# One-hot counts by groups of five destinations in a graph attention and expert kernel

## The reference

```
h = layernorm(x) @ W + b_w
e = leaky_relu(s_dst[dst] + s_src[src] + b_a);  w = exp(e)     # one score per edge
out[n] = sum of w * h[src] over the edges into n, divided by the sum of w
x = x + out
x = x + two of eight experts per node, weighted (hidden 256, gelu)
```

## Time and profile before

| | us |
|---|---|
| median of three runs | 764.05 |
| the profiled execution | 764.43 |
| its span, first to last instruction | 762.7 |
| PE busy | 676.3 |
| DVE busy | 549.9 |
| ACT busy | 461.4 |
| POOL busy | 284.8 |

### The profile page before, as it was taken

One profiled execution on the slowest core, in us unless ns is written; L12 is line 12 of the kernel. 1 busy time (PEld: TensorE's weight loads), 2 busy tenths in 40 slices (PEclk: granted clock), 3 DMA queues, 4 the chain that ended last, 5 costly groups with the idle time before them and its releaser, 6 DMA issues.

```text
span 762.7 us, 15157 instructions
## 1 busy us (share of the span) xinstructions
PE 676.3 (89%) x3518; PEld 527.3 (69%) x3519; DVE 549.9 (72%) x1510; ACT 461.4 (60%) x1227; POOL 284.8 (37%) x427
## 2 busy tenths in 40 slices
PE   3579964999999999999999999998789999999992
PEld 2457752777777777777777777776448788888881
DVE  4997778999998889989898989852694333333331
ACT  2245886788877888777777767720544455545551
POOL 2156720022222222222221212212233877777764
PEclk9798987999999999999999999999789999999997
DMA  8153000000010010101010101002912777777766
GB/s 321 48 181 126 1 1 1 16 29 29 29 57 29 25 33 28 56 28 55 29 55 29 55 29 55 29 29 98 390 50 57 139 130 133 132 127 130 138 121 81
DMA packets 29078, 59.72 MB, mean 78 GB/s; under 512 B 3792, under 2 KB 8272, under 8 KB 28752
## 3 DMA queue, kind: packets, MB, share of 16 engines
q0 software_dynamic: 10176, 24.12, 17.4%
q1 hardware_dynamic: 18400, 34.37, 12.6%
q10 hardware_dynamic: 432, 0.52, 0.2%
HBM read 35.93 MB, written 23.07 MB: 77 GB/s over the span
## 4 chain that ended last, share of the span: by engine, by line
PE 50%; DMA 10%; issue 6%; DVE 4%; POOL 2%; POOLq 2%; ACT 0%; DVEq 0%
PE ps L782 10%; PE ps L796 10%; PE ps L783 10%; DMA out_dram<-y,si 9%; PE ps L741 7%; PE ps L886 3%; PE ps L900 2%; PE ps L768 2%; PE ps L752 2%; PE ps L827 1%; PE ps L761 1%; PE ps L876 1%; DVE hot_r L1537 1%; POOLq L603 1%; POOL xg L623 1%
## 5 line engine op out<-in xcount | busy, mean ns | idle before, releaser
L1022 ACT ACTIVATE weight<-sdst_b,ss 128x125 f32 (+1 forms) x380 | 112.5, 388 | 84.1 <-DVE A_lo L1368 84.1
L782 PE MATMUL ps<-H_hi,A_hi 128*125 128x512 f32 x400 | 161.3, 403 | 0.9 <-DVE x_all L1382 0.9
L783 PE MATMUL ps<-H_lo,A_hi 128*125 128x512 f32 x400 | 157.9, 395 | 0.0
L1307 DVE TENSOR_SCALAR hot_k<-lane_k,key_t 128x250 bf16<-128x250 bf16 x600 | 121.0, 283 | 2.2 <-DVE weight_sum L1356 0.2
L532 POOL TENSOR_SCALAR seed<-seed 128x1 f32<-128x1 f32 x20 | 4.2, 212 | 308.7 <-DVE seed L1409 308.7
L1030 ACT ACTIVATE weight<-weight,ss 128x125 f32<-128x125 f32 x380 | 114.0, 388 | 0.0
L796 PE MATMUL ps<-H_hi,A_lo 128*125 128x512 f32 x400 | 105.0, 402 | 0.0
L782 PEld LDWEIGHTS ps<-H_hi,A_hi 128*125 128x125 f32 x400 | 74.2, 185 | 18.6 <-DVE x_all L1382 1.4
L783 PEld LDWEIGHTS ps<-H_lo,A_hi 128*125 128x125 f32 x400 | 74.3, 186 | 17.0
L886 PE MATMUL ps<-W_e,xgT 128*128 x352 | 83.4, 380 | 0.0
L796 PEld LDWEIGHTS ps<-H_hi,A_lo 128*125 128x125 f32 x400 | 71.5, 186 | 15.9
(11 more groups left out here) (238 smaller groups left out, 1186.6 us busy)
## 6 DMA issues: line engine op xcount, KB each, us to landing
W_e<-in_L_ffn_W_dram SPq DMA_DIRECT2D x16, 512.0 KB, 4.5
xf<-in_x_cols_dram SPq DMA_DIRECT2D x10, 512.0 KB, 3.8
x_all<-in_x_dram SPq DMA_DIRECT2D x20, 256.0 KB, 4.0
out_dram<-x_all SPq DMA_DIRECT2D x20, 256.0 KB, 2.0
xn_table<-xn SPq DMA_DIRECT2D x20, 256.0 KB, 2.3
b_b<-in_L_ffn_b_dram SPq DMA_DIRECT2D x1, 2048.0 KB, 8.9
Wf<-in_L_gnn_W_dram SPq DMA_DIRECT2D x1, 1024.0 KB, 6.1
b_b<-in_L_ffn_b_dram SPq DMA_DIRECT2D x1, 1024.0 KB, 13.8
```

The costliest lines, as they stand in the source:

```text
L782: pe.matmul(ps_agg[0:TN, :], A_hi[:, k, :], H_hi[:, k, :], start=(k == 0), stop=False)
L783: m = pe.matmul(ps_agg[0:TN, :], A_hi[:, k, :], H_lo[:, k, :], start=False, stop=False)
L1022: m = nc.scalar.activation(weight[s][:, k, :], dst_scores, ACT.Relu, bias=ss[:, 0, k:k + 1])
L1307: return nc.vector.tensor_scalar(into, lane_k[:, :], float(HW * h), key, ALU.add, ALU.is_equal)
```

## The change

Counts are made by groups ("windows") of five destinations, 25 to a tile and 500 in all. Each window has one slot of 128 edges, and one matmul of 100 columns (5 destinations by 20 source tiles) counts it. A tile with a window of more than 128 edges has its slots emptied and is counted chunk by chunk by the extra path. The slots are filled during the feature products: DVE searches each window's first chunk, POOL gathers that chunk for 500 windows (4 indirect loads of 125 rows of 128 edges), DVE finds the first edge in it, POOL gathers 128 edges from there (4 more), and DVE, PE (transposes) and ACT bring source lane and key of all slots into `lo2` and `key2`, lanes down, windows across. Per tile DVE then writes `hot_l` and `hot_k` with one comparison each. The additions over the source tiles go from DVE to POOL. PE counts 24 windows ahead of a tile's sums and the 25th, with the extra path's branch, after five pairs of them; the count of tile 1 moves behind the high part of tile 0, those of tiles 2 and 3 go into the high parts of tiles 1 and 2, and tile 1's sum goes to another PSUM bank. ACT makes its score copies between the high weights of tile 0. The loads of the edges move behind ACT's first feature copy.

```diff
+    WN = 5
+    WIN = TN // WN
+    WC = WN * NT
...
+            def window_rows(k):
+                pool.wait_ge(idx_ok, k + 1)
+                for g in range(WG):
+                    nc.gpsimd.indirect_dma_start(
+                        out=rows_w[0:WP, g, :, :].rearrange("p e j -> p (e j)"), out_offset=None, in_=edge_rows,
+                        in_offset=bass.IndirectOffsetOnAxis(ap=row_idx[0:WP, k, g:g + 1], axis=0)).then_inc(got_rows, 16)
...
                 if u >= 2:
                     low_rows(u - 2, u % 2)
+                if u == 2:
+                    window_rows(0)
+                if u == 4:
+                    window_rows(1)
...
+            def sums_of(t, s):
+                pool.wait_ge(A_ok, t + 1)
+                nc.gpsimd.tensor_tensor(tree[:, :, :], weight[s][:, 0:NT // 2, :], weight[s][:, NT // 2:NT, :], ALU.add)\
+                    .then_inc(tree_ok, 1)
+                for n, some in enumerate((5, 2, 1)):
...
+                nc.gpsimd.tensor_tensor(weight_sum[:, s, :], tree[:, 0, :], tree[:, 4, :], ALU.add).then_inc(sum_ok, 1)
...
                 if has(t, 1):
                     rstd_of_tile(t - 1, 1 - s)
+                if has(t, -1):
+                    sums_of(t + 1, 1 - s)
...
@@ PE
                 products(u)
+                if u == 0:
+                    chunk_rows()
+                if u == 2:
+                    window_edges()
+                if u == 3:
+                    dead_windows()
+                if u == 5:
+                    window_slots()
...
+            def window(w, stop):
+                at = w % WB * WC
+                return pe.matmul(ps_count[w // WB][:, at:at + WC], hot_l[:, w, :], hot_k[:, w, :],
+                                 start=(w % WB == 0), stop=stop)
...
+                pe.wait_ge(pairs_ok, t + 1)
+                for w in range(WIN - 1):
+                    window(w, w % WB == WB - 1)
...
+                counts_at = {0: NT, 1: 14, 2: 8}.get(t, 0) if peeled else 0
+                if has(t, -1) and counts_at == 0:
                     count(t + 1)
...
+                        if k and k == counts_at:
+                            count(t + 1)
+                        if k == counts_at + 5 and has(t, -1):
+                            count_rest(t + 1)
...
@@ ACT
+                if isinstance(t, int) and t == -1:
+                    for b in range(4):
+                        copy_group(b)
+                    for q in range(2):
+                        high_weights(0, 0, q)
+                    copy_group(GROUPS - 1)
+                    for q in range(2, 4):
+                        high_weights(0, 0, q)
...
+                    relus(1, 1)
@@ DVE
+            def pair_keys(t):
+                shape = [P, WIN, WC // 2, 2]
+                return nc.vector.tensor_tensor(
+                    hot_k[:, :, :].rearrange("p w (n j) -> p w n j", j=2),
+                    lane_c[:, :].rearrange("p (n j) -> p n j", j=2).unsqueeze(1).to_broadcast(shape),
+                    key2[:, bass.ds(WIN * t, WIN), :].unsqueeze(2).to_broadcast(shape), ALU.is_equal).then_inc(pairs_ok, 1)
...
+                if u == 0:
+                    first_chunks()
                 if u == 1:
-                    chunk_table()
+                    first_edges()
+                if u == 2:
+                    tile_table()
+                if u == 4:
+                    window_keys()
+                if u == 5:
+                    edge_keys()
...
-                    fold(t + 1, 1 - s, 0)
...
+                    if has(t, -2) and not (isinstance(t, int) and t == -1):
+                        pair_lanes(t + 2)
                 if here:
                     reciprocal_of(t, s)
-                if has(t, -2):
-                    dve.wait_ge(key_ok, t + 3)
-                    dve.wait_ge(sum_ok, t + 2)
-                    pairs_of(t + 2, at, range(HALVES))
+                if has(t, -2) and not (isinstance(t, int) and t == -1):
+                    pair_keys(t + 2)
```

More of the change, by code:

```diff
@@ L659, in _ @@
         def _(pe):
-            regs = [pe.alloc_register(f"pe_word{k}") for k in range(WORDS - 1)]
+            regs = [pe.alloc_register("pe_word")]
             def products(u):
@@ L708, in _, with scores_of_group @@
                     dst_scores(ps_d0[:, 0:TN], 0).then_inc(d0_ps, 1)
-            for b in range(GROUPS):
-                last = b == GROUPS - 1
-                pe.wait_ge(s_dst_ok, NT // 2 if last else NT // 2 - 1)
+            def scores_of_group(b):
+                pe.wait_ge(s_dst_ok, NT // 2 if b == GROUPS - 1 else NT // 2 - 1)
                 if b < len(ps_d):
@@ L786, in tile_products @@
                         if k == NT // 2:
-                            if not (isinstance(t, int) and t < 1):
+                            if not (peeled and t < 1):
                                 pe.wait_ge(den_ok, t)
@@ L791, in tile_products @@
                                 .then_inc(den_ps, 1)
-                if has(t, 0):
+                    if counts_at == NT:
+                        count(t + 1)
+                        count_rest(t + 1)
                     for k in range(NT):
@@ L795, in tile_products @@
                             pe.wait_ge(A_lo_ok, 4 * t + k // (NT // 4) + 1)
-                        m = pe.matmul(ps_agg[0:TN, :], A_lo[:, k, :], H_hi[:, k, :], start=False, stop=(k == NT - 1))
+                        m = pe.matmul(into, A_lo[:, k, :], H_hi[:, k, :], start=False, stop=(k == NT - 1))
+                        if k == NT // 4 and has(t, -2):
+                            words_of(pe, regs, t + 2)
                         if k == NT // 2 and has(t, 2):
@@ L1009, in _, with copy_group @@
             exps_0(range(16, 20), 5).then_inc(exp_ok, 1)
-            for b in range(GROUPS):
+            def copy_group(b):
                 act.wait_ge(d_ps, b + 1)
@@ L1137, in _ @@
         def _(dve):
-            regs = [dve.alloc_register(f"dve_word{k}") for k in range(WORDS)]
+            regs = [dve.alloc_register(f"dve_word{k}") for k in range(5)]
             n_dv = [0]
@@ new lines, in first_chunks @@
+            def first_chunks():
+                dve.wait_ge(max_ps, 1)
+                for g in range(WG):
+                    link(nc.vector.scalar_tensor_tensor(out=span[:, :], in0=ps_chunk, scalar=thr[:, g:g + 1],
+                                                        in1=chunk_1[:, :], op0=ALU.is_ge, op1=ALU.mult))
+                    link(nc.vector.tensor_reduce(found[:, g:g + 1], span[:, :], AX.X, ALU.min))
+                nc.vector.tensor_scalar(row_idx[:, 0, :], found[:, :], float(FAR), 2.0 * P, ALU.add, ALU.mult)\
+                    .then_inc(idx_ok, 1)
@@ L1416, in tile_step @@
                     add_x(t - 1, 1 - s)
+                if ahead and not (isinstance(t, int) and t == -1):
+                    extra_pairs(t + 1)
                 for q in range(4):
```

448 lines of the change are left out of this document (251 added, 197 removed).

## The result

The changed kernel takes **713.12 us** (median of four runs, 711.99 to 714.98), the kernel before 763.58 in the runs beside it: a ratio of 0.934, 95% interval 0.932 to 0.937, 50 us less. The forecast was 705 (692 to 730), faster. The profiled execution took 714.98 us with a span of 713.2, and what follows is read from it.

The account below looks back on a forecast made before the run. PE's own list was taken to bound the sixteen tiles. From the profiled 764.43 us, -12.9 before those tiles and -46 in fifteen steps gave 705.5, stated as 705, with a range of 692 to 730.

Parts of the forecast that it names:

- The fifteen steps: Steps with a count in tiles 4 to 19: 17.6 us each against 20.66, -46 us in all (ends -17 and -55).
- the gap at the branch: PE's pause before the last five counts of a step, 0.58 us before: taken as 0.25, between 0 and 0.58.
- the loop's edge: PE's pause at the loop's end, 0.49 us every second step before: stays, 0.25 on average.
- The 25 counts: Counting matmuls of 100 columns in a step: 52 ns each, 1.3 us together, between about 1.0 and 2.9.
- POOL's adds: Adds over source tiles on POOL: 6.9 us a step, done with 9 us to spare before PE wants them.
- the exclusion: POOL and DVE shut each other out in a step: costed at nothing; as a loop 31 us back, 736, chance 0.13.
- Tiles 0 to 3 then hang on ACT: First four tiles: tile 1's relus start only at 121, each tile takes ACT 15.8; 69.3 us against 70.7.
- The start: Up to the first product: it starts at 17.5 us, 9.8 earlier, or 6 earlier at the least.
- The products: Feature products with search and gathers: 90 us, ending at 107.5, 8.4 later than before, 8 either way.
- a dearer search: Rival in the product stage: gathers 4 us later per set and PE at its lower clock, 15 us, 720; chance 0.12.
- The first sum behind the products: Filling the tile pipeline: 12.5 us from the products' end to the first sum, at 120, 11.5 earlier.
- The fill's term: Everything before the sixteen tiles: they start at 189.3 instead of 202.2, -12.9 us (ends -3 and -22).

Follow-up runs that it names:

- e6: Changed kernel with the branch and the 25th count right behind the other 24 counts in every tile but the first two: 705.44 us.
- e5: Changed kernel with 24 of each tile's 25 counts issued twice, the sums staying the same: 727.17 us.
- e2: Changed kernel with the sums over sources of tiles 0 to 2 alone on DVE, the other seventeen on POOL: 706.70 us.
- e10: Changed kernel with gathers ahead of low rows and sums ahead of roots on POOL, and the 25th count right behind the others: 696.80 us.
- e1: Changed kernel with the sums over sources of all tiles back on DVE, right behind the weighing: 709.65 us.
- e12: Changed kernel with gathers first, 25th count behind the others, the first-edge search later, and all twenty tiles summed on DVE behind the one-hots: 698.03 us.
- e3: Changed kernel with the gathers of edge rows ahead of the low rows on POOL's list: 705.06 us.

## Why the prediction was right, and where it was not

- **The fifteen steps: right, and a little small.** 15 x (20.66 - 17.0) = 55 us instead of 46. The terms that were too large are the gap at the branch and the loop's edge (0.25 each, measured none: e6 and the steady step) and the low part (6.15, measured 5.99: its last row ends at 221.63 as it did before, 6.15 after its start, but the next count starts ahead of that end). The 25 counts at 1.3 came out at 1.28, in part by luck: a count costs 45 ns and not 52 (e5), and the 1.28 is the wait for the PSUM bank, which the forecast had as its lower end, at "about 1.0".
- **DVE and ACT in the step: right.** DVE from 17 to 10.4 busy us, ACT waiting 1.4 us.
- **POOL's adds: right on the steady step, wrong on the fill.** 5.5 us of adds a step against 6.9; the exclusion runs both ways, but the sum is there 5 us early. The step that failed is the one on the fill, "Tiles 0 to 3 then hang on ACT ... I get 69.3": there is no slack of 9 us in the fill, since nothing runs ahead yet, and the adds came on the path. PE waits 8.4 us for them, and the lower clock behind the waits costs an estimated 5 more; the stage is 8.3 longer than forecast. With three of the sums on DVE (e2) it is 6.1 shorter. With the chain shortened (e10) the sums of tiles 0 to 3 take 71.9 to the start of tile 4's sum, 70.6 to its counts, near the forecast's 69.3, and PE then waits more for ACT's high weights (2.7 us) than for sums (1.1).
- **The start: right.** 18.1 against 17.5.
- **The products: mechanism right, size short by 6.1.** The waits were 8.7 and 4.0 us against 9 and 3. DVE's work was 80.5 us against 77, among it the cast of 3.72 us (2.23 in e10) and the subtraction of 1.74, in both of which DVE stands for POOL. The three operations of 512 elements behind the cast, with no POOL beside them, take 0.41 to 0.43 each, and the subtraction runs on for 0.5 behind POOL; so an estimated 4.5 of the 80.5 us are such waits. The forecast counted the exclusion in the steady step but not here, and held against a dearer search that "POOL has nothing else to do then". Another 1.2 us of waits for PE and ACT, and small gaps make up the rest. The lower granted clock (0.87, before 0.91) is not behind it: DVE waits 0.7 us for PE in the whole stage.
- **The first sum behind the products: right**, 12.6 against 12.5.
- **The experts** took 237.0 instead of 234.8; in the profiles of e1 to e12 this stretch is 235.0 to 238.2 with no order that I can see. It stays open.

The fill's term, -12.9, thus came out at +2.3, outside its own bounds (-3 to -22). The steps' surplus of 8 made good about half of that miss, so that the total lay just within the forecast's own 697 to 714. That the two had opposite signs was luck.

## What to carry to other kernels

A slack read from a steady step says nothing about the first steps of a pipeline, where the same work stands on the path: cost an engine swap there by itself. Moving the adds to GpSimd did not pay here, as VectorE had room: the same adds on VectorE leave the step as it was (e1, e12), and the two engines hold each other up where they meet. And look at what a blocking instruction stands in front of: the three edits of order that gave 16 us (e10) remove no work at all.

## What the runs showed of the hardware that was not expected

- DVE and POOL wait for each other by whole operations. POOL's 1250-element add takes 2.40 us while DVE stands, and 3.92 where it starts beside DVE's `hot_l` compare: it ends at 128.90, 2.26 after that one. The 2500-element compare behind it, 1.47 in the steady step, takes 3.66 there and ends 1.32 after the add. A subtraction on one partition (1x500) ends 0.5 us after what POOL runs, whether it takes 1.74 us by that or 5.25. The page "SBUF — State Buffer" of the Trainium skill, section Who interferes with whom, has this as an exclusive lock; these rows agree.
- A matmul of 100 columns in bf16 with its own 128x128 weights costs 45 ns in a running list at a granted clock of 1.00 (e5).
- The branch around a path that isn't run costs PE nothing that can be measured here, ten matmuls behind the counts or right behind them (e6).
- The granted clock can fall to the lower level behind a wait of PE of 2.3 to 3.7 us (the changed kernel's tiles 0 to 2, 0.50) and need not (e3's tile 1, 1.00 with a wait of 2.53).
